# Product P2 of the pair products made by seven inner products in a ternary feed-forward kernel

## The chip, the cores and the metric

The kernel runs on one core of a Trainium2 chip. The metric is the device time of one execution in microseconds (us); the median of several executions is taken. Weights, inputs and outputs lie in the chip's memory (HBM). The core's engines are TensorE (PE, matmuls into PSUM banks), VectorE (DVE), ScalarE (ACT), GpSimd (POOL) and SyncE (SP), which issues most of the DMAs.

## The reference

```python
# x: (64, 64, 1024) f32; cond_128: (64, 128) f32
h = gelu(cond @ W0 + b0); h = gelu(h @ W1 + b1)
att = softmax(h @ W2 + b2)                               # (64, 8)
agg_w = einsum('bk,koi->boi', att, weight); agg_b = att @ bias_k
y = einsum('boi,bih->boh', agg_w, x) + agg_b[:, :, None]  # (64, 64, 1024)

def bitlinear(x, w):
    scale = mean(abs(w))
    q = round(clip(w / (scale + 1e-5), -1, 1))            # -1, 0 or 1
    return x @ (q * scale).T

out = x + bitlinear(bitlinear(y, w_gate) * bitlinear(y, w_up), w_down)
# w_gate, w_up: (2752, 1024); w_down: (1024, 2752)
```

The output is (64, 64, 1024) f32.

## The kernel before, in words

The 4096 tokens are worked on in eight chunks of 512, counted by `c` from 0 to 7. A first part computes the attention weights, sums and quantises the three weight matrices to -1, 0 and 1 in fp8, and transposes them on TensorE (line 761). Chunk 0 runs plainly (`group`, `down`), while the weights arrive. From chunk 1 (`FIRST`) on the work is done with the Strassen-Winograd scheme: the 2752 hidden rows are taken as ten pairs of 256 rows and a rest (`NPR` = 10, `NS` = 11 steps with the last, narrower one), and gate and up product of a pair are made together by seven products P1 to P7 instead of eight. A product takes a quarter of the input (512 contraction rows by 256 tokens, `operand`), split into two f16 parts, high and low, and a quarter of a pair's weights in fp8 (`ring`), for gate and up (h = 0, 1). That is 2 x 4 x 2 = 16 matmuls of 256 columns on line 881 (`product`). The weights' quarters and their sums were computed once in chunk 0, stored to the DRAM buffer `wcomb`, and are read back for every chunk, pair by pair, into three ring slots (`ring_load`, line 552).

P1, P6, P7 and P4 of a pair add up in one PSUM bank (`PB`), P5 and P3 in another (`PC`), P2 stands alone in `PA` = ps4. Between the products ScalarE copies the partial sums out (`copy_p1`, `copy_p16`, `copy_p167`, `gate21`; lines 1241, 1248, 1255, 1263). VectorE adds the banks to these copies (`c11`, line 1675, from P2 and the copy of P1; `c22`, line 1697; `c12`, line 1711), multiplies gate by up (`i11`, `i22`, `i12`, `i21`), forms the four sums of the result for the down products (`sums3`, `sum4`) and splits results into f16 parts (`lo_a`, line 1740; `lo_s`, line 1745, with ScalarE's `hi_blocks` and `hi_sums`). The order on each engine is written out by hand; semaphores order the engines among one another. On TensorE a pair's order is P1, P2, P4 of the pair before, a conv, P6, P5, P3 of the pair before, P7.

Two down stages (`down_group`, line 938) follow pair 5 and the last step. Their product banks are ps0 to ps5; VectorE adds each to the output rows in `xr` (`output2`, line 1762). A later stage adds the same bank again, after its output was read. Beside the second one VectorE and ScalarE scale and split the input of the next chunk (`scale_y`, `sum_quarter`, `lo_quarter`, `hi_quarters`).

The next chunk's input is prepared during pairs 2 to 9: `conv(c + 1, p - 2)` on TensorE applies the aggregated weights to x, which lies in `xa` (f32). `xa` is one buffer. Before x of the next chunk can be loaded (`next_x`, line 496), this chunk's x must have been copied to `xr` by ScalarE, in four `residual` copies (line 1043), two in pair 0 and two in pair 1. Then SyncE loads x, the bias, and, each when its ring slot is free (P3 of the pair three earlier is done), the pairs' weights. Chunks 2 to 6 are one loop; chunk 1 and chunk 7 are written out; chunk 7 has no next input (`more` is false).

## Time and profile before

| | us |
|---|---|
| median of 3 runs | 1728.03 (1727.51 to 1728.21) |
| span of the profiled execution, first to last instruction | 1726.1 |
| TensorE matmuls, busy | 1707.7 |
| VectorE, busy | 1096.0 |
| ScalarE, busy | 575.6 |
| GpSimd, busy | 28.0 |

The profile is of one execution. The trace holds its span alone; its own time outside the span is not recorded, and 1.9 us lie between the span and the median of the three runs. The granted clock of TensorE is 0.999 in the mean over the span. The busy time of an engine says how long at least one instruction of it was under way. Matmuls overlap: the duration of one (273 ns at 256 columns) is longer than the distance from one start to the next, and it is the distance that counts. In the rows, a time in brackets is the idle time of the engine before the instruction, with what ended it. A DMA's time to landing counts from its issue to its last byte.

### The profile page before, as it was taken

To read this page: it belongs to the slowest core of one execution; us is meant where nothing else is said; L and a number is where in the kernel's file an instruction comes from. 1 tells how busy PE (TensorE), PEld (TensorE's weight loads), DVE (VectorE), ACT (ScalarE), POOL (GpSimd) and SP (SyncE) were. 2 spreads that over 40 slices of the span, in tenths; PEclk is the share of its full clock that TensorE was granted. 3 is DMA by queue.
4 is the path that set the end of the run, shared out by engine and by line. 5 is a ranking of instruction groups with operands and counts; after the bars stand their busy time and mean duration, and the time that the engine had idled before them with its cause. 6 is when DMAs were issued, how large, how long until landed. Compare 5 with 4: busy or idle time off the path is not lost.

```text
span 1726.1 us, 31355 instructions
## 1 busy us (share of the span) xinstructions
PE 1707.7 (99%) x12424; PEld 1215.6 (70%) x12424; DVE 1096.0 (63%) x1786; ACT 575.6 (33%) x921; POOL 28.0 (2%) x59
## 2 busy tenths in 40 slices
PE   6999999999999999999999999999999999999999
PEld 5554545968769596795958768596776959678684
DVE  6898895555766468554685646755576545855464
ACT  6887732312333133230333213231233313323120
POOL 0010000000000000000000000000000000000000
PEclk9999999999999999999999999999999999999999
DMA  8666626312242032420224211331223313132021
GB/s 342 249 229 239 221 96 219 121 44 97 76 148 96 22 108 77 168 66 22 107 102 164 65 75 54 129 137 43 97 76 126 101 40 108 65 124 79 29 87 49
DMA packets 59735, 194.06 MB, mean 112 GB/s; under 512 B 5280, under 2 KB 5600, under 8 KB 59584
## 3 DMA queue, kind: packets, MB, share of 16 engines
q1 hardware_dynamic: 56432, 177.49, 28.9%
q0 software_dynamic: 2560, 14.36, 2.2%
q8 instruction: 109, 1.79, 0.4%
q14 instruction: 42, 0.34, 0.1%
q10 hardware_dynamic: 592, 0.09, 0.0%
HBM read 160.90 MB, written 31.01 MB: 111 GB/s over the span
## 4 chain that ended last, share of the span: by engine, by line
PE 97%; DVE 2%; DMA 1%; issue 0%; ACT 0%; SPq 0%; DVEq 0%
PE ps L881 52%; PE ps L938 25%; PE ps L658 17%; PE ps L899 2%; PE ps L761 1%; DMA xa<-in_x_dram 1%; DVE wsum L1318 0%; DVE ys L1413 0%; DVE msk L1458 0%; DVE ys L1380 0%; DVE xa L1529 0%; DVE prod L1496 0%; DVE yp L1418 0%; ACT wdT L1106 0%; SPq L493 0%
## 5 line engine op out<-in xcount | busy, mean ns | idle before, releaser
L881 PE MATMUL ps<-yp,wgT 128*128 128x256 f16 x4116 | 902.4, 273 | 1.1 <-issue 1.1
L881 PE MATMUL ps<-wuT,wgT 128*128 128x256 f16 x4116 | 902.4, 273 | 0.0
L881 PEld LDWEIGHTS ps<-yp,wgT 128*128 128x128 fp8e4 x4116 | 402.9, 98 | 50.8 <-issue 2.9
L881 PEld LDWEIGHTS ps<-wuT,wgT 128*128 128x128 fp8e4 x4116 | 402.7, 98 | 48.3
L938 PE MATMUL ps<-wdT,inter 128*128 128x512 fp8e4 x1960 | 433.2, 379 | 0.0
L938 PEld LDWEIGHTS ps<-wdT,inter 128*128 128x128 f16 x1960 | 191.1, 98 | 227.2 <-issue 1.4
L1762 DVE SCALAR_TENSOR_TENSOR xr<-ps,osc,xr 128x512 f32<-128x512 f32 x210 | 156.4, 748 | 168.2 <-PE ps L938 128.4
L1711 DVE TENSOR_TENSOR wdT<-ps,msk 128x512 f32<-128x512 f32 (+1 forms) x77 | 51.3, 666 | 207.1 <-PE ps L881 207.1
L1241 ACT COPY raw<-ps 128x512 f32<-128x512 f32 (+1 forms) x77 | 43.7, 567 | 314.6 <-PE ps L881 314.0
L1248 ACT COPY msk<-ps 128x512 f32<-128x512 f32 (+1 forms) x77 | 43.6, 567 | 138.1 <-PE ps L881 138.1
L1263 ACT COPY inter<-ps 128x256 f32<-128x256 f32 x70 | 26.1, 372 | 180.1 <-PE ps L881 180.1
L1745 DVE TENSOR_TENSOR inter<-inter 128x1024 f16<-128x1024 f32 x70 | 85.3, 1218 | 0.0
L1205 ACT CAST yp<-ys 128x1024 f16<-128x1024 f32 x49 | 48.5, 1042 | 102.0 <-DVE ys L1413 59.0
L1675 DVE TENSOR_TENSOR wdT<-ps,raw 128x512 f32<-128x512 f32 x70 | 48.4, 692 | 43.7 <-PE ps L881 43.1
L658 PE MATMUL ps<-yp,wgT 128*128 128x512 f16 x336 | 76.1, 379 | 0.0
L658 PE MATMUL ps<-yp,wuT 128*128 128x512 f16 x336 | 75.1, 379 | 0.0
L658 PE MATMUL ps<-wdT,inter 128*128 128x512 fp8e4 x336 | 73.8, 379 | 0.0
L1267 ACT CAST inter<-prod 128x768 f16<-128x768 f32 x35 | 29.1, 832 | 132.7 <-DVE prod L1715 132.7
L1271 ACT CAST inter<-inter 128x1024 f16<-128x1024 f32 x70 | 73.3, 1047 | 0.0
L1267 ACT CAST inter<-wuT 128x768 f16<-128x768 f32 x35 | 29.1, 832 | 127.7 <-DVE wuT L1715 127.7
L1697 DVE TENSOR_TENSOR wdT<-ps,raw 128x512 f32<-128x512 f32 (+1 forms) x77 | 50.8, 660 | 32.4 <-ACT raw L1255 32.4
L658 PE MATMUL ps<-ablk,xa 128*128 128x128 f32 x512 | 69.5, 282 | 0.6 <-DMA xa<-in_x_dram 0.3
(229 smaller groups left out, 1497.9 us busy)
## 6 DMA issues: line engine op xcount, KB each, us to landing
wgT<-wcomb SPq DMA_DIRECT2D x70, 896.0 KB, 4.7
wdT<-dcomb SPq DMA_DIRECT2D x14, 2240.0 KB, 10.9
xa<-in_x_dram SPq DMA_DIRECT2D x8, 2048.0 KB, 7.8
out_dram<-xr SPq DMA_DIRECT2D x64, 256.0 KB, 2.0
wcomb<-xa POOLq DMA_DIRECT2D x17, 448.0 KB, 3.0
xr<-in_L_ffn_w_down_dram SPq DMA_DIRECT2D x9, 512.0 KB, 5.5
inter<-in_L_ffn_w_gate_dram SPq DMA_DIRECT2D x7, 512.0 KB, 16.6
wdT<-in_L_ffn_w_up_dram SPq DMA_DIRECT2D x7, 512.0 KB, 4.4
```

The source lines that it names most:

```text
L658: return nc.tensor.matmul(o, l, r, start=start, stop=stop)
L881: last = nc.tensor.matmul(out, w, operand(i, OPERAND[what])[:, k, :], start=(start and h + k + i == 0), stop=(k == KQ - 1 and i == 1), ski ...
L938: last = nc.tensor.matmul(bank[:, :], x, wd_block(p, BLOCK[what]), start=(what in ("P1", "P2", "P5") and q + i == 0), stop=(q == GRP - 1 a ...
L1205: nc.scalar.copy(operand(0, s), quarter(s)).then_inc(s_yhi, 1)
L1241: nc.scalar.copy(t1[:, 0:w], PB[p % 2][:, 0:w]).then_inc(s_t1, 1)
L1267: nc.scalar.copy(pair_parts(p, 0, 0, 3), blocks4[p % 2][:, HALF:4 * HALF]).then_inc(s_hiA, 1)
L1271: nc.scalar.copy(pair_parts(p, 0, 3, 4), sums).then_inc(s_hiS, 1)
L1675: V.tensor_tensor(rr if p < NPR else g21, PA[:, 0:w], t1[:, 0:w], ALU.add).then_inc(s_c11, 1)
L1697: V.tensor_tensor(rr[:, TOK - w:TOK], PC[p % 2][:, 0:w], q67[:, 0:w], ALU.add).then_inc(s_c22, 1)
L1711: V.tensor_tensor(rr[:, 0:w], PC[p % 2][:, 0:w], q6[p % 2][:, 0:w], ALU.add).then_inc(s_c12, 1)
L1745: V.tensor_tensor(pair_parts(p, 1, 3, 4), sums, pair_parts(p, 0, 3, 4), ALU.subtract).then_inc(s_loS, 1)
L1762: V.scalar_tensor_tensor(xr[:, t, cols], bank[:, :], osc[:, t:t + 1], xr[:, t, cols], ALU.mult, ALU.add).then_inc(s_o, 1)
```

## The change

In chunks 2 to 7 (`later(c)`, the third chunk on), for the ten pairs, product P2 is no longer made by 16 matmuls of 256 columns. Its quarter of input and weights is quartered again, and the same scheme is used one level down: seven inner products of 256 contraction rows by 128 tokens by 256 weight columns (half gate, half up), each of 2 x 2 = 4 matmuls of 128 columns (`inner`, line 960 of the changed kernel). They are done in four steps: `inner_a` (two products), `inner_b`, `inner_g` (one each), and `inner_d` (three). The first three add into the first 128 columns of bank `IB` = ps5, the second product of `inner_a` stands beside them. ScalarE copies that sum out after each step, to PSUM bank `PA` or to `upper` in SBUF (`inner1`, `inner2`, `inner3`); VectorE adds the upper half into `PA` (`inner_upper`); then `inner_d` adds its three products on `PA`, which after that holds P2 as before.

The order on TensorE in a pair is now P1, inner_a, P4 of the pair before (in pair 0: the first half of P5), inner_b, a conv, first half of P6, inner_g, second half of P6, P5 (in pair 0: its second half), P3 of the pair before, inner_d, P7. On VectorE `c11` and `i11` of the pair move from before `i21` of the pair before to behind its `sum4`. On ScalarE the residual copies of pairs 0 and 1 move behind `copy_p16`.

The inner products need sums of the input quarter (`inner_sums`, `hi_inner`, `inner_lo`, beside the second down stage) and of the weights. GpSimd makes the latter once, in chunk 1, with four subtractions for each pair, and stores 128 KB for each pair in the DRAM buffer `wsub`. They are read back in every later chunk, into two buffers (`hi_r`, `sub1`) by the pair's parity (`sub_load`); those of pair 2 ahead of the next chunk's x. The load of the second half of the down weights moves from behind the ring load of pair 8 to behind that of pair 10.

```diff
@@ -114,6 +114,8 @@
+    INNER, TH = "P2", P
+    IA11, IA12, IS1, IS2, IS3, IS4, IA22 = range(7)
@@ -370,6 +374,22 @@
+        IB, isums = ps[5], sums.rearrange("p (s k n) -> p s k n", s=4, k=2)
+        upper = wu_flat[:, 4 * KH * TOK + 8 * TOK:4 * KH * TOK + 10 * TOK].bitcast(f32)
...
@@ -553,10 +579,22 @@
+            def sub_load(p):
+                dst = (hi_r[:, :].bitcast(f32), sub1[:, :].bitcast(f32))[p % 2]
+                sp.dma_start(dst, wsub[p]).then_inc(s_sub[p % 2], 16)
...
+                sub_load(1)
+                sp.wait_ge(s_ulo, UP * FIRST + 2 * (c - FIRST) + 1)
+                sub_load(0)
@@ -564,9 +602,14 @@
                 for p in range(RING, NS):
+                    if p > RING and not (isinstance(c, int) and c == FIRST):
+                        sp.wait_ge(s_m2, NS * (c - FIRST) + p - 2)
+                        sub_load(p - 1)
                     sp.wait_ge(s_m3, NS * (c - FIRST) + p - RING + 1)
+                    if isinstance(c, int) and c == FIRST:
+                        sp.wait_ge(s_subd, p - RING + 1)
                     ring_load(p)
-                    if p == 8:
+                    if p == NPR:
@@ -592,6 +635,9 @@
             def chunk(c):
+                if not (isinstance(c, int) and c == FIRST):
+                    sp.wait_ge(s_m2, NS * (c - FIRST) + 1)
+                    sub_load(2)
                 next_x(c)
@@ -648,6 +696,25 @@
             chunk(1)
...
+            for p in range(NPR):
...
+                nc.gpsimd.tensor_tensor(st[:, 0], uk[0], gk[0], ALU.subtract, saturate=False).then_inc(s_subt, 1)
...
+                nc.gpsimd.dma_start(wsub[p], p2[:, (p % 2) * HALF:(p % 2 + 1) * HALF]).then_inc(s_subw[p % 2], 16)
@@ -881,7 +951,53 @@
+            def inner(p, out, x, w, start=False):
+                for k in range(2):
+                    for i in range(2):
+                        last = nc.tensor.matmul(out, w[k], inner_x(i, x)[:, k, :], start=(start and k + i == 0),
+                                                stop=(k + i == 2), skip_group_check=True)
+                return last
...
+            def inner_a(c, p):
...
+                    pe.wait_ge(s_c11, n)
+                waited(c)
+                inner(p, IB[:, 0:TH], IA11, quarter_w(p, 0, 0), True)
+                inner(p, IB[:, TH:2 * TH], IS1, inner_sum_w(p, 0)).then_inc(s_ia, 1)
+
+            def inner_b(c, p):
+                pe.wait_ge(s_e1, NPR * (c - FIRST - 1) + p + 1)
+                waited(c)
+                inner(p, IB[:, 0:TH], IS2, inner_sum_w(p, 1)).then_inc(s_ib, 1)
+
+            def inner_g(c, p):
+                pe.wait_ge(s_e2, NPR * (c - FIRST - 1) + p + 1)
+                waited(c)
+                inner(p, IB[:, 0:TH], IS3, inner_sum_w(p, 2)).then_inc(s_ig, 1)
+
+            def inner_d(c, p):
+                pe.wait_ge(s_ir, NPR * (c - FIRST - 1) + p + 1)
+                waited(c)
+                inner(p, PA[:, 0:TH], IA12, quarter_w(p, 0, 1))
+                inner(p, PA[:, 2 * TH:3 * TH], IS4, quarter_w(p, 1, 1))
+                inner(p, PA[:, TH:2 * TH], IA22, inner_sum_w(p, 3)).then_inc(s_m2, 1)
@@ -992,6 +1110,25 @@
                         down_group(c, 0, more)
+                    if p < NPR and not (isinstance(c, int) and c == FIRST):
+                        product(c, p, "P1")
+                        inner_a(c, p)
+                        if p:
+                            product(c, p - 1, "P4")
+                        else:
+                            product(c, p, "P5", 0)
+                        inner_b(c, p)
+                        if more and p - 2 in range(KH):
+                            conv(c + 1, p - 2)
+                        product(c, p, "P6", 0)
+                        inner_g(c, p)
+                        product(c, p, "P6", 1)
+                        product(c, p, "P5", None if p else 1)
+                        if p:
+                            product(c, p - 1, "P3")
+                        inner_d(c, p)
+                        product(c, p, "P7")
+                        continue
                     product(c, p, "P1")
                     product(c, p, "P2")
@@ -1270,6 +1409,24 @@
+            def inner1(c, p):
+                act.wait_ge(s_ia, NPR * (c - FIRST - 1) + p + 1)
+                nc.scalar.copy(PA[:, 0:TH], IB[:, 0:TH]).then_inc(s_e1, 1)
+
+            def inner2(c, p):
+                act.wait_ge(s_ib, NPR * (c - FIRST - 1) + p + 1)
+                nc.scalar.copy(upper[:, 0:TH], IB[:, 0:TH]).then_inc(s_e2, 1)
+
+            def inner3(c, p):
+                act.wait_ge(s_ig, NPR * (c - FIRST - 1) + p + 1)
+                nc.scalar.copy(upper[:, TH:2 * TH], IB[:, 0:TH])
+                nc.scalar.copy(PA[:, TH:2 * TH], IB[:, 0:TH]).then_inc(s_e3, 1)
@@ -1279,13 +1436,22 @@
                 for p in range(NS):
+                    split = p < NPR and not (isinstance(c, int) and c == FIRST)
                     copy_p1(c, p)
-                    if p < 2:
+                    if split:
+                        inner1(c, p)
+                    if p < 2 and not split:
                         residual(c, 2 * p)
                         residual(c, 2 * p + 1)
                     if p:
                         gate21(c, p - 1)
+                    if split:
+                        inner2(c, p)
+                        inner3(c, p)
                     copy_p16(c, p)
+                    if p < 2 and split:
+                        residual(c, 2 * p)
+                        residual(c, 2 * p + 1)
@@ -1714,6 +1886,30 @@
+            def inner_upper(c, p):
+                dve.wait_ge(s_e3, NPR * (c - FIRST - 1) + p + 1)
+                V.tensor_tensor(PA[:, HALF:TOK].rearrange("p (a n) -> p a n", a=2),
+                                upper.rearrange("p (a n) -> p a n", a=2),
+                                IB[:, TH:2 * TH].unsqueeze(1).broadcast_to([P, 2, TH]), ALU.add).then_inc(s_ir, 1)
...
@@ -1816,7 +2019,7 @@
-                    if p < NPR:
+                    if p < NPR and not later(c):
                         c11(c, p)
                         i11(c, p)
@@ -1826,10 +2029,15 @@
+                    if p < NPR and later(c):
+                        inner_upper(c, p)
                     if p:
                         c12(c, p - 1)
                         i12(c, p - 1)
                         sum4(c, p - 1)
+                    if p < NPR and later(c):
+                        c11(c, p)
+                        i11(c, p)
```

ScalarE, pair 1 of the loop chunk, before. `msk` is the buffer of `copy_p16`, `raw` that of `copy_p1` and `copy_p167`, `xr<-xa` are the residual copies.

```order
L1241 COPY raw<-ps 128x512 [waits s_c11,s_m1]
L1043 COPY xr<-xa 128x1024 [waits s_st2,s_x]
L1043 COPY xr<-xa 128x1024 [waits s_st3,s_x]
L1263 COPY inter<-ps 128x256 [waits s_last,s_m4]
L1248 COPY msk<-ps 128x512 [waits s_m6]
L1266 ISA
L1267 CAST inter<-prod 128x768 [waits s_i12]
L1255 COPY raw<-ps 128x512 [waits s_c22,s_m7]
```

The same after. The copies of 128x128 are those of the inner products (`ps<-ps` to `PA`, `wuT<-ps` to `upper`).

```order
L1380 COPY raw<-ps 128x512 [waits s_c11,s_m1]
L1413 REGISTER_ALU
L1414 COPY ps<-ps 128x128 [waits s_ia]
L1402 COPY inter<-ps 128x256 [waits s_last,s_m4]
L1418 COPY wuT<-ps 128x128 [waits s_ib]
L1422 COPY wuT<-ps 128x128 [waits s_ig]
L1423 COPY ps<-ps 128x128
L1387 COPY msk<-ps 128x512 [waits s_m6]
L1180 COPY xr<-xa 128x1024 [waits s_st2,s_x]
L1180 COPY xr<-xa 128x1024 [waits s_st3,s_x]
L1405 ISA
L1406 CAST inter<-prod 128x768 [waits s_i12]
```

The two residual copies have moved from behind the first copy, which waits for P1 (`s_m1`), to behind the copy that waits for P6 (`s_m6`), and the four small copies stand ahead of them.

SyncE, head of the loop chunk, before. The first row waits for the residual copies (`s_xr`).

```order
L543 ISA [waits s_xr]
L496 ISA [waits s_y]
L496 DMA xa<-in_x_dram 128x4x1024
L506 ISA [waits s_ysc]
L506 DMA bbc<-biasd 128x512
L567 ISA
L552 DMA wgT<-wcomb 128x2x896 [waits s_m3]
```

The same after. `hi_r<-wsub` and `sub<-wsub` are loads of weight sums.

```order
L584 DMA hi_r<-wsub 128x256 [waits s_m2]
L568 REGISTER_ALU
L569 ISA [waits s_xr]
L522 ISA [waits s_y]
L522 DMA xa<-in_x_dram 128x4x1024
L532 ISA [waits s_ysc]
L532 DMA bbc<-biasd 128x512
L578 DMA wgT<-wcomb 128x2x896 [waits s_m3]
L606 REGISTER_ALU
L584 DMA sub<-wsub 128x256 [waits s_m2]
L578 DMA wgT<-wcomb 128x2x896 [waits s_m3]
```

The load of pair 2's sums, which waits for P2 of pair 0 (`s_m2`), stands ahead of the wait for the residual copies; from pair 3 on each ring load is followed by one load of sums.

## Rows read from the trace of the kernel before

**Rows 1.** the page: busy time of each engine; its chain by line
```profile
PE 1707.7 (99%) x12424; PEld 1215.6 (70%) x12424; DVE 1096.0 (63%) x1786; ACT 575.6 (33%) x921; POOL 28.0 (2%) x59
...
PE ps L881 52%; PE ps L938 25%; PE ps L658 17%; PE ps L899 2%; PE ps L761 1%; DMA xa<-in_x_dram 1%; DVE wsum L1318 0%; DVE ys L1413 0%; DVE msk L1458 0%; DVE ys L1380 0%; DVE xa L1529 0%; DVE prod L1496 0%; DVE yp L1418 0%; ACT wdT L1106 0%; SPq L493 0%
```

**Rows 2.** the chain in order of time (start us, us, what): one pair
```profile
730.76 12.23 PE ps L881 x112
```

**Rows 3.** TensorE in order of time, where a loop chunk begins
```profile
703.51 0.27 PE L881 MATMUL ps<-yp,wgT 128*128 128x256 f16 x1 [0.32 <-issue]
```

**Rows 4.** TensorE in order of time (start us, us), early transposes
```profile
101.11 0.61 PE L761 MATMUL ps<-identb,msk 128*128 128x128 bf16 x8
101.55 3.62 PE L658 MATMUL ps<-yp,wgT 128*128 128x512 f16 x16
105.01 0.61 PE L761 MATMUL ps<-identb,msk 128*128 128x128 bf16 x8
```

**Rows 5.** weight loads by shape: busy us, mean ns, idle before
```profile
L881 PEld LDWEIGHTS ps<-yp,wgT 128*128 128x128 fp8e4 x4116 | 402.9, 98 | 50.8 <-issue 2.9
...
L761 PEld LDWEIGHTS ps<-identb,msk 128*128 128x128 bf16 x256 | 17.4, 98 | 9.6 <-DVE msk L1458 0.8
```

**Rows 6.** ScalarE in order of time, pairs 0 and 1 of c = 3
```profile
705.45 0.59 ACT L1241 COPY raw<-ps 128x512 f32<-128x512 f32 x1 [13.08 <-PE ps L881]
...
714.18 0.59 ACT L1241 COPY raw<-ps 128x512 f32<-128x512 f32 x1 [1.16 <-PE ps L881]
714.67 1.99 ACT L1043 COPY xr<-xa 128x1024 f32<-128x1024 f32 x2
717.68 0.37 ACT L1263 COPY inter<-ps 128x256 f32<-128x256 f32 x1 [1.02 <-PE ps L881]
```

**Rows 7.** VectorE in order of time, end of pair 5 of c = 3
```profile
775.49 0.69 DVE L1711 TENSOR_TENSOR wdT<-ps,msk 128x512 f32<-128x512 f32 x1 [3.26 <-PE ps L881]
776.21 0.42 DVE L1715 SCALAR_TENSOR_TENSOR prod<-wdT 128x256 f32<-128x256 f32 x1
776.76 0.42 DVE L1736 TENSOR_TENSOR inter<-prod,inter 128x256 f32<-128x256 f32 x1
777.53 0.96 DVE L1740 TENSOR_TENSOR inter<-prod,inter 128x768 f16<-128x768 f32 x1 [0.35 <-ACT inter L1267]
...
779.13 0.42 DVE L1701 SCALAR_TENSOR_TENSOR wuT<-wdT 128x256 f32<-128x256 f32 x1
779.47 1.22 DVE L1745 TENSOR_TENSOR inter<-inter 128x1024 f16<-128x1024 f32 x1
```

**Rows 8.** TensorE in order of time, first down stage of c = 3
```profile
776.94 6.42 PE L938 MATMUL ps<-wdT,inter 128*128 128x512 fp8e4 x29
```

**Rows 9.** VectorE in order of time, second down stage of c = 2
```profile
700.42 0.75 DVE L1762 SCALAR_TENSOR_TENSOR xr<-ps,osc,xr 128x512 f32<-128x512 f32 x1 [0.92 <-PE ps L899]
```

**Rows 10.** GpSimd in order of time, around 282 us
```profile
282.54 0.39 POOL L270 COPY ablk<-aT 64x256 f32<-64x256 f32 x1
```

**Rows 11.** the DMA queue's issues in order of time, c = 3
```profile
716.96 0.40 SPq L496 DMA_DIRECT2D xa<-in_x_dram  x1
717.57 0.35 SPq L506 DMA_DIRECT2D bbc<-biasd  x1
722.91 96.18 SPq L552 DMA_DIRECT2D wgT<-wcomb  x6
```

**Rows 12.** line 496 (load of x), its five issues from 500 us on
```profile
DMA to landing us min/median/max: 7.6/7.7/7.8
```

**Rows 13.** tile xa, 690 to 920 us: duration ns min/median/max, first and last start
```profile
L658 PEld LDWEIGHTS ps<-ablk,xa x64: 190/192/192, 729.6 to 852.4; 128*128 128x128 f32 x64
L658 PE MATMUL ps<-ablk,xa x64: 275/275/275, 729.7 to 852.5; 128*128 128x128 f32 x64
```

**Rows 14.** line 552 (ring load), its three issues in 866 to 875 us
```profile
DMA to landing us min/median/max: 4.6/4.7/6.5
```

**Rows 15.** line 506 (bias load), its five issues from 500 us on
```profile
DMA to landing us min/median/max: 7.6/7.8/7.9
```

More of the change, by code:

```diff
@@ L831, in down, with product @@
                 last.then_inc(s_dn, 1)
-            def product(c, p, what):
+            def product(c, p, what, half=None):
                 n = NS * (c - FIRST) + p
@@ L837, in product @@
                 bank = PA if what == "P2" else (PC if what in ("P5", "P3") else PB)[p % 2]
-                if what == "P1":
+                if half == 1:
+                    pass
+                elif what == "P1":
                     pe.wait_ge(s_ring[p % RING], 16 * ((4, 4, 3)[p % RING] * (c - FIRST) + p // RING + 1))
@@ L872, in product @@
                     pe.wait_ge(s_c22, n + 1)
-                if p == 0:
+                if p == 0 and half != 1:
                     pe.wait_ge(s_ylo, KH * c + OPERAND[what] + 1)
-                waited(c)
-                for h in range(2 if p < NPR else 1):
+                if half != 1:
+                    waited(c)
+                for h in range(2 if p < NPR else 1) if half is None else (half,):
                     out = bank[:, h * HALF:(h + 1) * HALF]
@@ L912, in down_group @@
                             pe.wait_ge(s_i21, n + NPR)
+                        elif not (isinstance(c, int) and c == FIRST):
+                            pe.wait_ge(s_ir, NPR * (c - FIRST - 1) + GRP + 1)
                     if what in AFTER:
@@ L1615, in sum_quarter @@
                     dve.wait_ge(s_ylo, KH * c + A12 + 1)
+                    if not (isinstance(c, int) and c == FIRST):
+                        dve.wait_ge(s_isum, 4 * (c - FIRST))
                     V.tensor_tensor(quarter(S4), quarter(A12), quarter(S2), ALU.subtract).then_inc(s_sy, 1)
@@ L1671, in c11 @@
                 elif p:
-                    dve.wait_ge(s_i22, NPR * (c - FIRST) + p)
+                    dve.wait_ge(s_i12 if later(c) else s_i22, NPR * (c - FIRST) + p)
                 elif later(c):
@@ L1692, in c22 @@
                 dve.wait_ge(s_q67, n + 1)
-                if p:
+                if later(c) and p < NPR:
+                    dve.wait_ge(s_i11, NPR * (c - FIRST) + p + 1)
+                elif p:
                     dve.wait_ge(s_i12, NPR * (c - FIRST) + p)
@@ L1706, in c12 @@
                 dve.wait_ge(s_q6, n + 1)
-                if p < NPR - 1:
+                if later(c) and p < NPR:
+                    dve.wait_ge(s_i22, NPR * (c - FIRST) + p + 1)
+                elif p < NPR - 1:
                     dve.wait_ge(s_i11, NPR * (c - FIRST) + p + 2)
@@ L1724, in sums3 @@
                 dve.wait_ge(s_i21, NS * (c - FIRST) + p + 1)
+                if p == 0 and later(c):
+                    dve.wait_ge(s_ilo, c - FIRST)
                 if p or later(c):
@@ L1769, in tail @@
                 if more:
+                    if not later(c):
+                        for i in range(2):
+                            dve.wait_ge(s_subw[i], 16 * (NPR // 2))
                     scales(c + 1)
@@ L1788, in tail @@
                         (("scale", 6), ("scale", 7)), (("sum", S1), ("lo", A11)), (("lo", A21),), (("sum", S3),), \
-                        (("sum", S2),), (), (("lo", A12),), (("sum", S4),), (("lo", A22),), (("lo", S1),), (("lo", S2),), \
-                        (("lo", S3),), (("lo", S4),)
+                        (("sum", S2),), (("inner", 0),), (("lo", A12),), (("sum", S4),), (("lo", A22),), (("lo", S1),), \
+                        (("lo", S2),), (("lo", S3), ("inner", 1)), (("lo", S4),)
                 for d in range(len(DOWN[1])):
@@ L1796, in tail @@
                                 scale_y(c + 1, k)
+                            elif what == "inner":
+                                (inner_sums, inner_lo)[k](c + 1)
                             elif what == "sum":
```

81 lines of the change are left out of this document (80 added, 1 removed).

## The prediction

> **What bounds the kernel now.** I read the page's busy line and its chain first. TensorE is busy 99% of the span, and the chain that ended last is nearly all TensorE: 52% line 881, the matmuls of the pair products, 25% line 938, the down products [rows 1]. So time is saved by taking columns off TensorE, and lost where a wait opens in front of it. Next the chain in order of time: a pair's 112 matmuls of line 881 take 12.23 us [rows 2], so one 256-column matmul takes 109.2 ns, without a hole. The only hole per loop chunk is 0.32 us of issue at the loop's return [rows 3], which stays. VectorE (63%) and ScalarE (33%) have room on average, so the question is only whether a handover comes too late for TensorE. For that I read their rows and the DMA queue's in the first pairs of the chunk that starts at 703.51. (Chunks are counted by c, 0 to 7, as in the code.)
>
> **The columns.** From c = 2 on there are six chunks with ten pairs, 60 products P2. Each had 2 halves x 4 k-blocks x 2 parts = 16 matmuls of 256 columns: 16 x 109.2 = 1.747 us. Now it has 7 inner products x 2 k-blocks x 2 parts = 28 matmuls of 128 columns, each with its own weight load. The pair products have no such matmul before, so I bound one. The nearest rows are the transposes of line 761: 128 x 128, 2-byte operands, a weight load each, between full-rate matmuls. From group to group it is 3.90 us (101.11, 105.01); the 16 matmuls of 512 columns between take (3.62 - 0.38) / 15 = 0.216 us each, 3.456 together; the rest, 0.446 us, is eight transposes, 55.8 ns each [rows 4]. The other end is a weight load's own length, 98 ns, for the transposes and for line 881 alike [rows 5]; if loads could not overlap each other, 28 would cost 2.74 us. But the transposes have the same load and still go at 55.8, so I take 55.8: 28 x 55.8 = 1.562 us. Saved per pair: 0.185 us; in 60 pairs **11.1 us**.
>
> The Trainium skill, TensorE: Matmul & The Clock Gate, section Back-to-back issue gap, states that a sustained stream of weight-load and matmul pairs at 128 columns runs at about 81 ns a matmul, against some 56 for an isolated gap. By that, 28 would take an estimated 2.27 us, 0.52 us more than now, and the change would cost an estimated 31 us. The trace agrees with the lower figure (55.8), but only over runs of eight; the change has runs of 8, 4, 4 and 12.
>
> **The handovers inside a pair.** The bank of the inner products now passes from TensorE to ScalarE and back between them. Pair 1 starts at 703.51 + 80 x 0.1092 = 712.25, its third product (P4 of pair 0) ends 3 x 1.747 later, at 717.49, and ScalarE's copy of it starts at 717.68, 0.19 behind [rows 6]. That copy, 256 columns, takes 0.37 us; the 512-column one takes 0.59 and lets the next start 0.10 before its end (714.18, 714.67), so a 128-column copy takes some 0.26 and the 256-column one frees the engine after 0.27. With t for the end of P4, the copy behind inner_b runs from t + 0.46 to t + 0.72; inner_g is due after inner_b and half of P6, t + 0.22 + 0.87 = t + 1.09: slack 0.37 us. In pair 0, with P5's first half between, the copy of P1 starts 1.94 us into the chunk (705.45), that of inner_a at 2.43, and ends at 2.69 against 3.07. Even a copy as long as the 512 form would end before inner_g is due. A smaller slack than this is met now without a hole: line 1740 ends at 778.49 [rows 7], and the matmul that needs it is the ninth of the down stage that starts at 776.94 [rows 8], due at 778.67. PSUM as target of a copy has no row; its ends are nothing and the 512 form's 0.59. Pairs with a conv behind inner_b have 0.89 us more. I take 0, with 0 to 2 us for the 20 pairs without one (0 and 1 of five chunks, all of c = 7).
>
> VectorE gets one 256-column addition per pair, 0.42 us like its others [rows 7]; it is done about 7.5 us into the pair, and TensorE wants it at 10.5. The sum of P1 and P2 (c11) moves behind that of P3: it starts 0.5 us before the pair ends, is done 0.2 after, and inner_a wants it 1.75 us into the next. The place with the least slack is the first down stage, whose ninth matmul wants line 1740 of pair 4. P3 now ends 0.67 us earlier against that stage, for the 12 matmuls of inner_d come behind it, and c11 and i11 of pair 5 come in between: 775.49 - 0.67 + (0.72 + 0.55 + 0.34) + (0.72 + 0.34) = 777.49, against 777.53 now [rows 7]. Cost 0. The four sums and the split for the next chunk (about 1.6 and 1.2 us on VectorE, 1.05 on ScalarE) stand in the second down stage, where VectorE waits 0.92 us before each of its last outputs [rows 9]: 0. GpSimd's 40 operations fall into c = 1; a copy of 64x256 costs it 0.39 us [rows 10], and even at 1 us each a pair's four fit into 13.1 us; so do ten stores, and 60 loads of 128 KB beside 896 KB per pair, each issued a pair ahead: 0.
>
> **The next input.** This is the moved step that costs. In pair 1 ScalarE's residual copies stood right behind the copy of P1; now they stand behind the copy of P6. The load of x waits for them, since it overwrites their source. Before: residuals from 714.67 to 716.66 [rows 6], x issued at 716.96 [rows 11], 0.30 later, landing after 7.7 us [rows 12], at 724.7; the conv that needs it starts its weight load at 729.6 [rows 13]: 5 us of cover. Now, from pair 1's start s: P6 ends at s + 1.747 + 0.446 + 1.747 + 0.223 + 0.874 + 0.223 + 0.874 = s + 6.13; its copy starts 0.19 later, the residuals 0.49 after that and end 1.99 later, at s + 8.80; x is issued at s + 9.10 and lands at s + 16.80. The conv is due after one pair (96 x 0.1092 + 1.562 = 12.05) and P1, inner_a, P4, inner_b (4.16): s + 16.21. So x is 0.59 us late, and the conv's weight load, 0.19 us [rows 13], comes only behind it: 0.78 us. Five chunks, c = 2 to 6, load a next input: **3.9 us lost**. The third pair's sums are loaded ahead of it about 6.8 us into the chunk, while the queue waits anyway: that edit costs 0.
>
> **The sum.** -11.1 + 3.9 = -7.2 us. The profiled execution's span is 1726.1 us, 1.9 under the median of 1728.03; what lies around it stays. So 1718.9 for the span, 1720.8 for the time.
>
> **The rivals.**
> (a) The input is in time after all. For it: I find only 0.59 us of lateness out of 16. Against it: its landings are very even, 7.6 to 7.8 us [rows 12]. Gives 1728.0 - 11.1 = 1716.9.
> (b) The input comes much later. The ring load of pair 3 is issued when P3 of pair 0 ends, at s + 9.8, now right behind x and no longer 6 us after it [rows 11]. If they share the engines, x is held up as the later of two ring loads was, 6.5 against 4.7 us [rows 14]: 1.8 us, in five chunks 9 us, 1729.8; at 2.2 us, 1731.8, just slower. It decides from 1.4 us of hold-up on, where the gain is gone. Against it: the bias load, an eighth of x and issued 0.6 us behind it, takes 7.8 us too [rows 15], so it lands after x and not before: the queue works in order.
> (c) Short matmuls run at the pace of their weight loads. At 98 ns, 28 x 0.098 - 1.747 = 1.0 us more a pair, 60 in all: 1728 + 60 + 4 = 1792, **slower**. It decides from 60 ns on: the input's 3.9 us leave 0.12 us of the 0.185 a pair, 4 ns on each of 28. For it: runs of 12 have no row. Against it: eight in a row at 55.8 with the same load.
> (d) The handovers eat some: up to 2 us on ScalarE, or an unseen 0.1 us in every pair, 6 us: 1721 to 1727.
>
> **How the numbers follow.** Forecast 0.60; (a) 0.16; (d) 0.09; (b) 0.08; (c) 0.07. Within 0.2% is 3.5 us either way, about what a measurement of this kernel can tell from no change. The forecast, (a) and half of (d) are faster: 0.80. The rest of (d) and half of (b) are within: 0.09. The rest, 0.11, is slower. The range goes from just below (a), 1716, to the upper end of (d), 1727; (b) and (c), 0.15, are left out.
>
> **What would show it.** Line 960 with 1680 matmuls whose starts lie 55.8 ns apart; pairs of the last chunk 12.05 us long against 12.23; TensorE idle 0.6 to 0.9 us before the first conv of each of the five chunks, released by the DMA of xa; no idle before inner_b, inner_g or inner_d. I am wrong if those starts lie over 60 ns apart, if TensorE waits for ScalarE between inner products, or if the wait for x is nothing or over 2 us.

## The result, and the profile after

The changed kernel takes 1730.78 us in the median of 16 runs (1727.64 to 1736.19), the kernel before 1727.63 us in 16 runs beside them (1727.17 to 1729.76). The ratio is 1.0019, interval 1.0012 to 1.0026: slower, by little but clear of no change, where 1720.8 and faster was forecast. The columns were saved as worked out. They were spent again at the load of the next input, which comes 1.1 us later than forecast in every loop chunk, and at the entry of the convolutions, which the prediction did not price; the median holds some time at half clock besides.

The page of the changed kernel, its busy line and its chain by engine and by line, against [rows 1]:

```profile
PE 1702.7 (99%) x13136; PEld 1218.7 (71%) x13144; DVE 1126.7 (65%) x1876; ACT 634.9 (37%) x1167; POOL 62.5 (4%) x109
...
PE 94%; DMA 3%; ACT 1%; DVE 1%; issue 1%; SPq 0%; ACTq 0%; DVEq 0%
PE ps L951 43%; PE ps L1056 25%; PE ps L725 18%; PE ps L960 5%; DMA xa<-in_x_dram 3%; PE ps L1015 2%; PE ps L828 1%; ACT xr L1180 1%; ACT msk L1198 0%; DVE msk L1624 0%; DVE ys L1546 0%; DVE xa L1695 0%; DVE prod L1662 0%; ACT wdT L1243 0%; SPq L519 0%
```

TensorE is busy 5 us less than before, and the span is 1728.4 us, 2.3 more. The load of x has gone from 1% to 3% of the chain, and the residual copies ahead of it (line 1180) stand in the chain now.

From the view of TensorE's waits (engine, line, what released it, us in total, times, longest):

```profile
PE ps L725 <- DMA xa<-in_x_dram: 8.8, 6, 1.8
...
PE ps L725 <- ACT msk L1198: 3.0, 1, 3.0
```

Before, the wait for x was 0.3 us, once, for the first input. One of the five new waits, TensorE in order of time, c = 3:

```profile
732.49 1.15 PE L725 MATMUL ps<-ablk,xa 128*128 128x128 f32 x8 [1.66 <-DMA xa<-in_x_dram]
```

From the start of the last matmul ahead of it to the start of this one, 1.87 us more pass in the mean than the 0.056 us between two of the inner matmuls, 9.34 us in five chunks: the wait and the weight load of 0.19 us behind it. The same place answers to [rows 6, 11] here, ScalarE and the DMA queue of c = 3:

```profile
718.87 0.27 ACT L1418 COPY wuT<-ps 128x128 f32<-128x128 f32 x1
719.92 0.27 ACT L1422 COPY wuT<-ps 128x128 f32<-128x128 f32 x1 [0.78 <-PE ps L960]
...
720.79 0.58 ACT L1387 COPY msk<-ps 128x512 f32<-128x512 f32 x1 [0.44 <-PE ps L951]
721.28 1.99 ACT L1180 COPY xr<-xa 128x1024 f32<-128x1024 f32 x2
```
```profile
723.57 0.39 SPq L522 DMA_DIRECT2D xa<-in_x_dram  x1
724.16 0.35 SPq L532 DMA_DIRECT2D bbc<-biasd  x1
724.56 0.43 SPq L578 DMA_DIRECT2D wgT<-wcomb  x1
725.11 0.43 SPq L584 DMA_DIRECT2D sub<-wsub  x1
```

Issued as worked out, 9.1 us into pair 1. But the landing of line 522's five loads, against [rows 12], is not:

```profile
DMA to landing us min/median/max: 8.8/8.8/8.9
```

The matmuls of the inner products came out as forecast. TensorE in order of time, last chunk, the twelve matmuls of inner_d between P3 and P7 (line 960, then line 951 again):

```profile
1661.95 0.22 PE L960 MATMUL ps<-yp,wgT 128*128 128x128 f16 x1
1662.01 0.22 PE L960 MATMUL ps<-wuT,wgT 128*128 128x128 f16 x1
...
1662.57 0.22 PE L960 MATMUL ps<-wuT,hi_r 128*128 128x128 f16 x1
1662.62 0.27 PE L951 MATMUL ps<-yp,wgT 128*128 128x256 f16 x1
```

The twelfth start after 1661.95 is at 1662.62: 0.67 / 12 = 55.8 ns each. The runs of four and of eight go at the same distance. The chain in order of time has the pair's length, here in the last chunk and in c = 6 (start us, us, what):

```profile
1365.52 4.37 PE ps L951 x40
...
1378.51 4.37 PE ps L951 x40
...
1543.23 4.37 PE ps L951 x40
...
1555.28 4.37 PE ps L951 x40
```

Without a convolution a pair takes 1555.28 - 1543.23 = 12.05 us, the forecast to the digit, and the last chunk is 1.83 us shorter than before. With one, it takes 12.99. Before, in the same chunk:

```profile
1360.41 12.23 PE ps L881 x112
1373.53 12.23 PE ps L881 x112
```

13.12 us, so only 0.13 are saved and not 0.185. The other 0.05 us are lost at the convolution, of which there are 40. TensorE in order of time, the eight matmuls of a convolution that waits for nothing, the kernel before first:

```profile
742.82 1.06 PE L658 MATMUL ps<-ablk,xa 128*128 128x128 f32 x8
```
```profile
745.52 1.11 PE L725 MATMUL ps<-ablk,xa 128*128 128x128 f32 x8
```

The second of the eight starts 165 ns behind the first where it was 112. An f32 weight load takes 192 ns, an fp8 one 98, and ahead of a convolution now stand four matmuls of 55.8 ns (inner_b) in place of sixteen of 109.2; my reading is that they leave the f32 loads less of a lead, and the second experiment below bears on it. In 35 convolutions that is 53 ns each. In the five that wait for x the second starts 208 ns behind the first, 96 more than before. Together 2.3 us.

So the loads and the entries account for the columns: -11.1 + 9.3 + 2.3 = +0.5 us. The hole at the loop's return [rows 3] did not stay as forecast: over its four returns it was 1.1 us before and is 0.5 now, which leaves about 0. The profiles show +0.15: their spans differ by 2.3 us, and 2.15 of these lie ahead of chunk 1, in code that is alike in both. Busy times and granted clock (the column after POOL) in the same 6.9 us of the changed kernel, then in 5.3 us of the kernel before:

```profile
36.30:43.20 6.90, 6.09 (x14) 1.70 (x14) 5.03 (x9) 4.63 (x11) 0.00 (x0) 0.51 0.65 254
```
```profile
36.70:42.00 5.30, 4.34 (x20) 1.64 (x20) 4.68 (x13) 3.85 (x9) 0.00 (x0) 1.00 0.78 305
```

Half level (1.2 GHz) against full (2.4), around the end of the same wait (3.0 us, above; 3.16 before). Which execution gets it varies: a second profile of the changed kernel has none there, and six profiles of other versions have one. Over all executions the time goes with the mean granted clock: 1736.19 us at 0.994 and 1727.64 at 0.999, a difference of 8.6 us for 0.5% of the span. The changed kernel's three executions with a mean clock of 0.999 (two of the 16, one of 11 later ones) took 1727.64, 1728.22 and 1728.49 us, level with the kernel before.

### The profile page after: what moved, and what is told of

Read it like the earlier page. It is cut to its first block, busy times and chain, and to the rows that moved or that the text cites. A ratio compares the mean times of both kernels' runs of the same rounds, so it can differ in the third digit from the quotient of the medians.

```text
span 1728.4 us, 33623 instructions
## 1 busy us (share of the span) xinstructions
PE 1702.7 (99%) x13136; PEld 1218.7 (71%) x13144; DVE 1126.7 (65%) x1876; ACT 634.9 (37%) x1167; POOL 62.5 (4%) x109
## 4 chain that ended last, share of the span: by engine, by line
PE 94%; DMA 3%; ACT 1%; DVE 1%; issue 1%; SPq 0%; ACTq 0%; DVEq 0%
PE ps L951 43%; PE ps L1056 25%; PE ps L725 18%; PE ps L960 5%; DMA xa<-in_x_dram 3%; PE ps L1015 2%; PE ps L828 1%; ACT xr L1180 1%; ACT msk L1198 0%; DVE msk L1624 0%; DVE ys L1546 0%; DVE xa L1695 0%; DVE prod L1662 0%; ACT wdT L1243 0%; SPq L519 0%
## 5 line engine op out<-in xcount | busy, mean ns | idle before, releaser
L951 PE MATMUL ps<-yp,wgT 128*128 128x256 f16 x3636 | 808.4, 273 | 0.5 <-issue 0.2
L951 PE MATMUL ps<-wuT,wgT 128*128 128x256 f16 x3636 | 808.5, 273 | 0.0
L951 PEld LDWEIGHTS ps<-yp,wgT 128*128 128x128 fp8e4 x3636 | 355.8, 98 | 42.6 <-issue 2.4
L951 PEld LDWEIGHTS ps<-wuT,wgT 128*128 128x128 fp8e4 x3636 | 355.8, 98 | 40.6
L1056 PEld LDWEIGHTS ps<-wdT,inter 128*128 128x128 f16 x1960 | 191.3, 98 | 227.0
L725 PEld LDWEIGHTS ps<-ablk,xa 128*128 128x128 f32 x512 | 64.7, 198 | 11.9 <-issue 9.4
L725 PEld LDWEIGHTS ps<-wdT,inter 128*128 128x128 f16 x336 | 32.9, 98 | 39.4
```

Of the source, the lines that this page charges most:

```text
L725: return nc.tensor.matmul(o, l, r, start=start, stop=stop)
L951: last = nc.tensor.matmul(out, w, operand(i, OPERAND[what])[:, k, :], start=(start and h + k + i == 0), stop=(k == KQ - 1 and i == 1), ski ...
L1056: last = nc.tensor.matmul(bank[:, :], x, wd_block(p, BLOCK[what]), start=(what in ("P1", "P2", "P5") and q + i == 0), stop=(q == GRP - 1 a ...
```

## The experiments

Each ran beside the kernel before, on the same chip as the others of its group.

### Which wait: the input or the convolution's entry (first group, before 1727.82)

**Residual copies all in pair 0.**

```diff
-                    if p < 2 and split:
-                        residual(c, 2 * p)
-                        residual(c, 2 * p + 1)
+                    if p == 0 and split:
+                        for t in range(NT):
+                            residual(c, t)
```

> All four residual copies stand in pair 0, behind the copy of P6, so x is issued about 10 us into the chunk and is there long before conv 0. In the changed kernel's profile TensorE loses 1.87 us before that conv in each of five chunks, 9.3 us. Theory W (the late input costs the wait, and the waits are what drops TensorE's clock in some executions): the five waits are gone, the median is the changed kernel's fastest run less 9.3, near 1718.3, and the executions lie within 1 us. Theory S (the clock losses belong to the start of the kernel, where the profile shows 6.8 us at half clock): the waits are gone too, but the median falls only by 9.3 to 1721.5 and the executions still spread over 8 us. Theory H (the moved copies hold up ScalarE's copies of P7, P1 or the inner products): TensorE waits in pair 1 and the time stays above 1722.

Measured: 1718.59 us (1718.45 to 1719.04, 5 runs), ratio 0.9946 (0.9933 to 0.996). x is issued at 712.01 in c = 3 and lands after 7.5 us (7.5 to 8.0 in the five chunks); TensorE waits nowhere for it in the loop. 12.2 us came back against the changed kernel's median: the 9.3 of the waits, and some 3 us by which that median lies over its fastest executions. The wait for the input is the main loss. That the 3 us hang on the waits too is suggested and not shown by this: the five executions here all lie within 0.6 us, at a clock of 0.998 or 0.999.

**Convolution behind the first half of P6.**

```diff
                         inner_b(c, p)
-                        if more and p - 2 in range(KH):
-                            conv(c + 1, p - 2)
                         product(c, p, "P6", 0)
+                        if more and p - 2 in range(KH):
+                            conv(c + 1, p - 2)
```

> Only the conv moves, from behind inner_b to behind the first half of P6. Theory C (the conv's first f32 weight load of 0.19 us does not fit behind the four 128-column matmuls of inner_b, which costs 0.06 us in each of 40 convs): 2.4 us less than the changed kernel, median near 1728.4, and the first conv matmul's distance falls from 165 to 111 ns. The rival, that the 165 ns belong to the conv's own wait or to its first matmul wherever it stands: no change, 1730.8. The x wait shrinks by up to 0.87 us in each of five chunks, since the conv is due later, but P6 then runs in that time: 4.4 us less in addition if x lands when it did, so 1724 in all; without theory C 1726.4.

Measured: 1722.08 us (1721.73 to 1724.4, 6 runs), ratio 0.9969 (0.9957 to 0.9981). TensorE in order of time, a convolution in pair 3 of c = 3:

```profile
742.18 1.06 PE L725 MATMUL ps<-ablk,xa 128*128 128x128 f32 x8
```

1.06 us again, as in the kernel before: where a convolution does not wait, the entry's cost is gone. The first of the chunk is due 0.87 us later and so waits half as long (0.93 instead of 1.87), with x still landing after 8.8 us. The entry's cost stays at the five that wait; the rest of it and the shorter waits are 6.5 us of the 8.7 by which the median fell. Two reasons for the entry's cost are not told apart by this: that the matmuls ahead are short, or that they are only four; here eight of 256 columns stand in their place.

**Both.**

> Both edits: residual copies in pair 0, conv behind the first half of P6. Theory W with C: 11.2 us of columns saved and nothing lost, 1727.6 - 11.2 = 1716.4, within 1 us in all executions, no TensorE idle in the loop beyond the 0.32 us at its return. Theory S: 1719 to 1720 with the spread of the changed kernel. Without C: 2.4 us more than that.

Measured: 1717.94 us (1716.43 to 1718.55, 5 runs), ratio 0.9939 (0.9926 to 0.9953). That is 1.5 us over what was expected and only 0.7 under the version with the residual copies alone. No wait for x is left; the profiled execution has 6.8 us at half clock around the wait ahead of chunk 1, which the other's has not. The fastest executions of the two differ by 2.0 us, near the entry's 2.3.

### Why x takes 8.8 us: its neighbours in the queue

**Ring load of pair 3 only after x has landed** (rival (b) taken away).

```diff
+                if not (isinstance(c, int) and c == FIRST):
+                    sp.wait_ge(s_x, 16 * (c + 2))
                 pairs(c)
```

> The residual copies stay late; the ring load of pair 3 and the weight sums behind it are issued only when x has landed. Theory Q (x takes 8.8 us and not 7.7 because the ring load issued 1 us behind it shares the DMA engines): x lands in 7.7 us, the wait before conv 0 falls from 1.87 to about 0.8 us, 5.4 us less in all, median near 1725.4, and fewer executions lose clock. The rival, that the bias load or the weight sums of pair 2 hold x up, which stay as they are: x still takes 8.8 us and the median stays at 1730.8.

Measured: 1730.25 us (1727.68 to 1733.71, 11 runs), ratio 1.0011 (1.0002 to 1.002). In c = 3 the ring load is issued at 734.56, behind the landing of x; x still takes this (line of the load of x, five issues):

```profile
DMA to landing us min/median/max: 8.7/8.8/9.1
```

So neither the ring load nor the sums behind it hold x up; rival (b) had about the right size for a wrong reason. The bias load right behind x stayed; it is just as close in the kernel before, where x takes 7.7.

### Why x takes 8.8 us: an instruction fetch (second group, before 1728.5; third group, before 1727.77)

The first two of these runs, and the two of the kernel before, are of the second group; the waits that were placed anew and their control are of the third.

The DMA packets of the changed kernel while x is in transit, by queue (packets, MB, share of 16 engines):

```profile
q1 hardware_dynamic: 698, 2.47, 84.7%
q8 instruction: 1, 0.02, 0.7%
```

In the kernel before, the same stretch (717.0 to 724.6) has only the first kind:

```profile
q1 hardware_dynamic: 659, 2.36, 85.8%
```

The odd packet is a fetch of instructions, 16,384 bytes, 0.94 us on one DMA engine (0.7% of 16 x 8.8). Between two such fetches lie about 250 instructions of TensorE (median 249 to 254 in the traces). In the loop of the changed kernel one starts 22.8 us into the chunk, and x is in transit from 17.7 on; in the kernel before, one starts near 10.0 and the next near 23.5 us, and x is in transit from 13.5 to 21.1, between them. The kernel before has such a case too, once: its load of x in chunk 1 has a fetch inside and takes 9.0 us.

The landings say how the 1.1 us come about. A load of x lands in 16 parts, and the trace has the time of each. In c = 3 of the changed kernel 15 parts are in after 7.07 to 7.58 us, and the last comes at 8.80; in the kernel before the 16 come at 7.15 to 7.68. So it is in all profiles: of a load that takes 8.7 us or more, 15 parts are in by 7.4 to 8.1 us, and one is 0.8 to 1.5 us behind. The load as a whole is not slower; one part of 16 is, as when one DMA engine had something else to do.

That it is the fetch is so far only a coincidence of times, so the fetch was moved without moving anything else, by repeating a wait that has long been met in TensorE's program ahead of the loop. The instructions behind shift by that many places against the blocks that a fetch brings.

**128 such waits in the changed kernel**, 64 before the first matmul and 64 before the wait of 3 us.

```diff
-            pe.wait_ge(s_ident, 2)
+            for _ in range(65):
+                pe.wait_ge(s_ident, 2)
...
+            for _ in range(64):
+                pe.wait_ge(s_ident, 2)
             pe.wait_ge(s_sum_act, sum(on_act[:NG - 5]))
```

> The changed kernel with 128 more waits on a semaphore that has long been reached in TensorE's program, half of them before its first matmul and half before the 3 us wait in the first chunk. They compute nothing; they move TensorE's instructions of all later loops by 128 places, so that its 16 KB instruction fetches come some 6.8 us earlier against its work (two fetches lie 13.6 us apart, 256 instructions). Nothing else moves: x, the bias, the ring load and the weight sums are issued as in the changed kernel. Theory F: no fetch falls inside the transit of x any more (it would come near 16 and 29.5 us of the chunk, x is in transit from 17.7 to 25.4), x lands in 7.7 us, TensorE's wait for x falls from 1.87 to about 0.8 us in each of five chunks, -5 us: 1725 to 1726, with a narrower spread. Rival (the hold-up is the crowd of transfers behind x, or the bytes in flight, and the fetch is a bystander): x still takes 8.8 us and the time stays 1730.

Measured: 1726.45 us (1723.66 to 1728.06, 11 runs), ratio 0.9986 (0.9977 to 0.9995). x lands in 7.7 to 8.0 us in four of five chunks; in those a fetch starts 0.3 to 0.4 us ahead of the issue of x, and the next one behind its landing. In c = 3 it takes 8.7, again with one part late, with no fetch in its midst; one starts 0.2 us ahead of its issue like the others, but takes 1.5 us where they take 1.0 to 1.2. Whether that is the reason no run here tells. The waits themselves cost 1.9 us at the start here (the first matmul comes at 6.12 us instead of 4.17).

**The changed kernel again**, beside it.

> The changed kernel once more, for the comparison on the same chip and for a second profile: theory F expects a fetch inside the transit of x and 8.7 to 9.0 us of landing in five chunks again, a wait for x of 1.8 to 1.9 us in each, 1728 to 1734 between executions. If some executions show the clock granted at half level right after such a wait or in the first 50 us, the spread between executions is the clock's, not the loads'.

Measured: 1730.06 us (1727.92 to 1733.83, 11 runs), ratio 1.001 (1.0001 to 1.0019), x in 8.75 to 9.0 us. This profile has no half-clock stretch around 40 us, but one right behind the wait of c = 3, from 731.8 to 735.2. TensorE at the wait's end, then the stretches around (clock after POOL):

```profile
730.84 1.24 PE L725 MATMUL ps<-ablk,xa 128*128 128x128 f32 x8 [1.85 <-DMA xa<-in_x_dram]
```
```profile
726.80:731.80 5.00, 3.15 (x32) 2.80 (x30) 2.99 (x6) 1.10 (x4) 0.00 (x0) 1.00 0.81 324
731.80:735.20 3.40, 3.40 (x20) 2.48 (x19) 1.12 (x2) 0.43 (x2) 0.00 (x0) 0.50 0.35 136
735.20:740.00 4.80, 4.80 (x52) 4.37 (x51) 0.81 (x2) 1.12 (x2) 0.00 (x0) 1.00 0.00 0
```

That chunk is 207.68 us long, 1.8 more than the next. Of the 20 waits of 1.6 to 2.0 us in four profiles (this one, the first, the ring load behind x, the control below) three were followed by such a stretch within 1.2 us; behind the 15 waits of 0.4 to 1.5 us in three other profiles there was none. Three in 20 against none in 15 is too little to say that the shorter waits are safe.

**128 waits placed so that they delay less** (42 and 86 in the two places).

> The changed kernel with 128 more waits on a reached semaphore, as in the run that moved the fetch, but 42 ahead of the first matmul and 86 ahead of the 3 us wait, so that they delay nothing (with 64 and 64 the first matmul came at 6.12 us instead of 4.17). Theory F: x lands in 7.7 to 8.0 us in at least four of five chunks, the wait for x is 0.8 us in each, and with the 1.9 us of the start back the time is 1724.5 (1722.5 to 1726.5). Rival (the 3.6 us by which the first of these runs beat the changed kernel were the chip's spread): 1730.

Measured: 1724.02 us (1722.84 to 1726.42, 11 runs), ratio 0.9981 (0.9972 to 0.999): faster than before. They were meant to delay nothing; the first matmul comes at 4.90 us instead of 4.17, here and in the control below. Line of the load of x, five issues; and the first convolution of c = 3:

```profile
DMA to landing us min/median/max: 7.5/7.6/8.0
```
```profile
728.51 1.15 PE L725 MATMUL ps<-ablk,xa 128*128 128x128 f32 x8 [0.48 <-DMA xa<-in_x_dram]
```

A fetch starts 0.3 us ahead of the issue of x in all five, the next one 12 us behind it. Wait and weight load together are 3.68 us in five chunks, 0.74 each; the prediction had 0.78.

**42 waits, all before the first matmul**: the control.

> The changed kernel with 42 more waits on a reached semaphore at the start of TensorE's program, where it waits for its first data anyway: TensorE's instruction fetches of the later loops come some 2.3 us earlier, near 20.6 us of a chunk instead of 22.9, still inside the transit of x (17.7 to 26.5). A control of the run in which 128 such waits moved the fetch out of it. Theory F: x still lands in 8.7 to 9.0 us, the wait for x stays 1.8 to 1.9 us, 1730 (1728 to 1733). Rival (the waits themselves, not the place of the fetch, brought the shorter landing): 7.7 to 8.0 us and 1725 to 1726.

Measured: 1729.26 us (1728.13 to 1734.69, 11 runs), ratio 1.001 (1.0001 to 1.0019), 5.2 us over the last. The fetch starts 5.0 to 5.6 us behind the issue of x, still inside, but not the 2.3 us earlier that I had reckoned: in the changed kernel it is 5.1 to 5.9. So a fetch that is due while x is in transit does not start when it is due. The packets of its transit in c = 3, its five landings, and the same convolution:

```profile
q1 hardware_dynamic: 692, 2.45, 81.5%
q8 instruction: 1, 0.02, 0.7%
```
```profile
DMA to landing us min/median/max: 8.8/8.9/9.0
```
```profile
733.02 1.15 PE L725 MATMUL ps<-ablk,xa 128*128 128x128 f32 x8 [1.74 <-DMA xa<-in_x_dram]
```

The same kind of instruction added, the same transfers, the same start: what differs for x is the place of the fetch. The fetch makes the 1.1 us.

**128 waits in the kernel before** (the first edit above).

> The same 128 waits in the kernel before. There no fetch lies inside the transit of x in five chunks (at 10.0 and 23.5 us of a chunk, x between 13.5 and 21.1); moved by about 6.8 us one comes near 16.7 us, inside. Theory F: x lands in 8.7 to 9.0 us instead of 7.7 in chunks c=2 to c=6, though nothing of the change is in this kernel; its time stays within 0.2% of before, since x is there 3 to 5 us ahead of the first convolution. Rival (fetches are bystanders): x lands in 7.7 us as before.

Measured: 1729.54 us (1728.99 to 1732.3, 10 runs), ratio 1.0011 (1.0002 to 1.0021), 1.0 us over the kernel before; its first matmul comes 1.9 us later, as above. In c = 2 to 6 the expectation was missed: x landed in 7.7 to 8.05 us. The fetch had not gone where I meant to put it, but started 7.5 to 7.7 us after the issue of x in four of the five, when x was all but in, and at 7.9 in the fifth, behind its landing. In c = 1 the shift took a fetch out of the transit: 7.65 us, where the kernel before has this (packets and landing in the transit, then the same in the kernel with the waits):

```profile
q8 instruction: 1, 0.02, 0.7%
...
xa<-in_x_dram SPq DMA_DIRECT2D x1, 2048.0 KB, 9.0
```
```profile
xa<-in_x_dram SPq DMA_DIRECT2D x1, 2048.0 KB, 7.6
```

**One part of the change alone: pair 1's residual copies behind the P6 copy, in the kernel before.**

```diff
-                    if p < 2:
-                        residual(c, 2 * p)
-                        residual(c, 2 * p + 1)
+                    if p == 0:
+                        residual(c, 0)
+                        residual(c, 1)
                     if p:
                         gate21(c, p - 1)
                     copy_p16(c, p)
+                    if p == 1:
+                        residual(c, 2)
+                        residual(c, 3)
```

> The kernel before, with one thing of the change alone: the two residual copies of pair 1 stand behind that pair's big f16 copy, so that x of the next input is issued about 5 us later in each chunk. Theory F (an instruction fetch inside the transit of x holds it up by about 1.1 us): in the kernel before a fetch lies 24 us into the chunk, x issued near 18.7 us would then land after about 8.8 us, at 27.5, and the first convolution, due near 26.2 us, waits about 1.3 us in each of five chunks: +6 to +8 us, 1734 to 1736, perhaps with a spread of some us between executions. Rival (the hold-up belongs to the weight-sum loads or the shorter matmuls of the changed kernel): x lands in 7.7 us, the wait is 0.3 us or less, +1 to +2 us, 1729. Rival (the position costs nothing, as nothing of the seven inner products is here): within 0.2%.

Measured: 1730.65 us (1729.59 to 1732.16, 11 runs), ratio 1.0012 (1.0003 to 1.0021). x is issued 18.7 us into the chunk and lands after 7.5 to 8.0 us; wait and weight load cost 1.67 us in five chunks. My theory had a fetch inside and 8.8 us. Again it started at the end of the transit or behind it (7.4 to 8.1 us after the issue), 26.0 to 26.6 us into the chunk, though the kernel before has it at 23.5 to 24.0. So a fetch that is due while x is in transit sometimes goes in its midst and sometimes only behind it. What decides that, no run here tells. That the moved copies cost time by themselves is shown: 2.1 us in the medians (0.5 to 3.6 by the interval), and in the trace the 1.67 with 0.5 more at the entries of the five convolutions that wait.

### The version that beats both, again

> The version with all four residual copies in pair 0 and the convolution behind the first half of P6, once more. If its gain is the columns (-11.1 us) plus handovers, and neither a wait for x nor clock lost after one, it is 1717 to 1718.5 again, ratio 0.993 to 0.995, in a profile without a wait for x in the five loop chunks.

Measured: 1716.89 us (1716.5 to 1717.21, 5 runs), ratio 0.9935 (0.9922 to 0.9949). In this profile x takes 8.7 us in two of the five chunks: in c = 3 with a fetch 5.0 us behind its issue, in c = 5 with none in its midst, and with one that starts 0.6 us ahead of its issue as in c = 6, where x takes 7.4. That one stays open. But x is issued 10 us into the chunk and there is cover: no wait. The chain has this pair length in c = 6:

```profile
1339.94 4.37 PE ps L951 x40
...
1352.88 4.37 PE ps L951 x40
```

12.94 us, 0.18 under the 13.12 of before: here the columns' whole gain arrives, and the median lies 10.9 us under the kernel before, of the 11.1 worked out.

## Why the prediction was wrong

- **The columns, -11.1 us: right.** 55.8 ns a matmul, 12.05 us a pair. Rival (c) fell: the runs of twelve (inner_d) go at 55.8 ns too. The figure of the Trainium skill (TensorE: Matmul & The Clock Gate, Back-to-back issue gap), about 81 ns for a sustained stream, was not met here.
- **The handovers, 0: right.** TensorE waits for nothing at inner_b, inner_g and inner_d; rival (d) fell in its form. The hole at the loop's return, which was to stay, shrank by 0.5 us in all; no run here says why.
- **The next input, +3.9 us: the step that failed.** The issue of x (9.10 us into pair 1), the time at which the convolution is due and the 0.19 of the weight load were right. Wrong was "lands after 7.7 us", a figure taken over from [rows 12]. Its narrow spread, 7.6 to 7.8, was no property of the load but of its place between two fetches. The rows began at 500 us and so left out a sixth load of the same size in the same trace, at 306.01, which took 9.0 us. I moved the load by 4 us inside the chunk and did not ask what else was there. It landed after 8.8: 9.3 us in place of 3.9. With the fetch out of the way the same code has 3.7. The argument against rival (a), that the landings are very even, rested on the same rows.
- **The convolution's entry, +2.3 us: missing in the sum.** The rows were there: 192 ns for the f32 weight load against 98 [rows 5, 13]. I had asked what the short matmuls do to each other, not how much of a lead four of them leave to the load behind. It matters little for one convolution, but there are 40.
- **Rival (b)** had +9 us from the input by the queue's sharing. The ring load issued after the landing changed nothing, so the mechanism fell though its number came near.
- **Clock.** The rest, up to 3 us of the median, goes with time at half clock (0.999 at 1727.64 us, 0.994 at 1736.19). Three profiles show some of it right behind a wait for x. That these waits make the executions spread over 8.6 us, where the kernel before spreads over 2.6, is argued from this and not shown. I had priced a wait at its length only.
- **The sum.** With the three corrections it reads -11.1 + 9.3 + 2.3 - 0.5 = 0, 1728.0 for the time; measured 1727.6 to 1728.5 at a mean clock of 0.999, 1730.8 in the median. The range's upper end, 1727, left out a miss of 1.1 us in one transfer, times five.

The DMA page of the Trainium skill (DMA: Bandwidth & Descriptors, Queues, rings and completion order) says that each DMA engine takes turns between the queues that have work for it, a packet at a time. The runs agree in this: a packet of 0.94 us on one of 16 engines goes with one of 16 parts that lands late, and makes the load 1.1 us longer, about the packet's length. The fetches that came only at the end of a transit do not look like taking turns.

## What to carry to other kernels

Before moving a load or a step by some microseconds, look at what lies at the new place in all queues, the instruction queue too: a steady landing time holds for its place. Where a wait of less than 1 us decides about a gain, give the load cover rather than reckon it exact: here two lines (the residual copies in pair 0) were worth 12 us in the median, 9.3 of them traced to the waits, as much as the whole change was to bring. And where short matmuls replace long ones, check the weight load of what follows them, by its own type.

## What the runs showed of the hardware

- TensorE's instructions come in by DMA, 16 KB at a time (0.94 us on one DMA engine). With one in the midst of a 2 MB load (4.6 to 5.9 us after its issue) the load takes 8.7 to 9.1 us, in 34 of 34 cases from chunk 1 on in all profiles; of the 44 loads without one there 42 take 7.4 to 8.1 and two 8.7. In the long ones 15 of 16 parts are in by 7.4 to 8.1 us and one comes 0.8 to 1.5 us behind. Loads of 896 KB showed nothing of it in the kernel before (median 4.7 us with a fetch inside and without); with the 128 waits in that kernel, 13 of 34 with a fetch inside took 5.7 to 6.2.
- 42 or 128 instructions that do nothing, put in once ahead of a loop, decide about 5 us of a kernel's time: 1729.26 against 1724.02.
- Behind four 55.8 ns matmuls f32 weight loads (192 ns) are not hidden: +53 ns at the second matmul of the convolution. Behind eight of 256 columns they are.
- After a wait of TensorE of 1.6 to 2.0 us for x the granted clock fell to half for 3.4 us in 3 of 20 cases, which cost about 1.7 us each; after the 15 waits of 0.4 to 1.5 us it did not.
